# Heads in pairs: scores of the next pair ahead of the transposes of this one, in a two-layer kernel on one core

## What is computed

```python
# layer 0, attention part
xn = rms_norm(x, g_norm) * (1 + scale_b) + shift_b
q, k, v = split(xn @ W_qkv)                  # 512 x 1536
q, k = rms_norm(q, g_q), rms_norm(k, g_k)    # over the 32 values of a head
attn = softmax(q @ k.T * 32 ** -0.5)         # 256 x 256 for each head
o = attn @ v
x1 = o + o @ W_out
# layer 0, feed-forward part, weights from 4-bit codes, scales and a rank-16 term
x2 = relu(x1 @ w_up + b_up) @ w_down + b_down
# layer 1: 256 steps of a Runge-Kutta recurrence with a 512 x 512 coupling,
# x2 as its drive, and a mixture of experts on its states
```

## Time and profile before

| | us |
|---|---|
| median of 3 runs | 2893.96 |
| lowest and highest of them | 2891.05, 2894.92 |
| the profiled execution's own time | 2898.88 |
| its span, from the first to the last instruction | 2897.1 |
| what lies around the span | 1.8 |
| layer 0, to about | 870 |
| layer 1, from there | 2027 |

### The profile page before, as it was taken

One profiled execution on the slowest core, in us unless ns is written; L12 is line 12 of the kernel. 1 busy time (PEld: TensorE's weight loads), 2 busy tenths in 40 slices (PEclk: granted clock), 3 DMA queues, 4 the chain that ended last, 5 costly groups with the idle time before them and its releaser, 6 DMA issues.

```text
span 2897.1 us, 132208 instructions
## 1 busy us (share of the span) xinstructions
PE 2714.9 (94%) x49688; PEld 2397.8 (83%) x49696; DVE 1806.4 (62%) x6366; ACT 1139.6 (39%) x4994; POOL 1364.0 (47%) x3476
## 2 busy tenths in 40 slices
PE   7487988888899999999999999999999999999998
PEld 5265766676687778999999999999999999999987
DVE  4665675565565556666666666666666666666654
ACT  3343345456544333334334333333433433433322
POOL 2422001112116665665666666666666666666600
PEclk8699999999999998999999999999999999999999
DMA  7622344344420003444444444444444444444376
GB/s 218 203 70 70 95 131 144 114 154 159 140 91 3 4 28 98 129 131 131 132 127 135 128 130 129 136 127 127 136 127 129 134 132 128 130 134 130 117 236 201
DMA packets 138459, 363.74 MB, mean 126 GB/s; under 512 B 15968, under 2 KB 25312, under 8 KB 137696
## 3 DMA queue, kind: packets, MB, share of 16 engines
q1 hardware_dynamic: 137568, 357.06, 40.1%
q10 hardware_dynamic: 672, 3.67, 0.3%
HBM read 324.62 MB, written 34.47 MB: 124 GB/s over the span
## 4 chain that ended last, share of the span: by engine, by line
PE 60%; POOL 5%; issue 3%; DVE 2%; DMA 0%; ACT 0%; POOLq 0%; DVEq 0%; SPq 0%
PE pscan L1504 12%; PE pd L1457 12%; PE pg L1409 12%; PE pscan L1500 12%; PE pu L1409 11%; POOL lin L1254 1%; POOL lin L1270 0%; POOL from_q L1266 0%; POOL carry L1299 0%; POOL lin L1264 0%; POOL lin L1276 0%; POOL from_q L1272 0%; POOL from_q L1281 0%; POOL lin L1285 0%; PE prouter L1519 0%
## 5 line engine op out<-in xcount | busy, mean ns | idle before, releaser
L1500 PEld LDWEIGHTS pscan<-th,carry 128*128 128x128 f16 x16384 | 551.1, 96 | 71.7 <-ACT th L1319 50.4
L1500 PE MATMUL pscan<-th,carry 128*128 128x8 f16 x16384 | 560.3, 166 | 19.5 <-ACT th L1319 8.7
L1504 PE MATMUL pscan<-th,carry 128*128 128x16 f16 x16384 | 558.2, 169 | 1.6 <-DVE th L1615 1.1
L1504 PEld LDWEIGHTS pscan<-th,carry 128*128 128x128 f16 x16384 | 482.3, 96 | 2.8 <-DVE th L1615 2.1
L1319 ACT ACTIVATE th<-state 128x32 f16<-128x32 f32 x768 | 175.9, 229 | 688.5 <-DVE state L1632 688.5
L1457 PE MATMUL pd<-hg,wbuf 128*128 128x256 f16 x3168 | 429.3, 274 | 2.6 <-DMA wbuf<-w_split 2.6
L1409 PE MATMUL pg<-qh,wbuf 128*128 128x256 f16 x3168 | 427.3, 274 | 0.0
L1409 PE MATMUL pu<-qh,wbuf 128*128 128x256 f16 x3168 | 423.1, 272 | 0.0
L1632 DVE TENSOR_REDUCE state<-pscan 128x32 f32<-128x96 f32 x768 | 197.7, 257 | 263.2 <-PE pscan L1504 257.4
L1409 PEld LDWEIGHTS pg<-qh,wbuf 128*128 128x128 f16 x3168 | 295.0, 98 | 36.6 <-issue 0.3
L1409 PEld LDWEIGHTS pu<-qh,wbuf 128*128 128x128 f16 x3168 | 292.4, 97 | 31.9
(11 more groups left out here) (273 smaller groups left out, 4774.7 us busy)
## 6 DMA issues: line engine op xcount, KB each, us to landing
wbuf<-w_split SPq DMA_DIRECT2D x264, 512.0 KB, 3.5
wbuf<-w_split SPq DMA_DIRECT2D x264, 384.0 KB, 3.1
parts_mem<-in_w_tiles SPq DMA_DIRECT2D x149, 256.0 KB, 3.2
w_split<-parts_mem SPq DMA_DIRECT2D x99, 256.0 KB, 2.8
late<-in_w_tiles SPq DMA_DIRECT2D x49, 256.0 KB, 3.5
w_split<-spare SPq DMA_DIRECT2D x33, 128.0 KB, 3.1
out<-oo SPq DMA_DIRECT2D x8, 512.0 KB, 3.6
w_qkv<-in_w_qkv ACTq DMA_DIRECT2D x1, 3072.0 KB, 10.0
```

The lines of the kernel that those rows point to most:

```text
L1500: mm(pscan[:, 0, m * B:(m + 1) * B], clo[:, k, m * P:(m + 1) * P], th[:, k, 0, :], start=(m == 0 and k == 0), stop=False, skip_group_check ...
L1504: ins = mm(pscan[:, 0:2, m * B:(m + 1) * B], chi[:, k, m * P:(m + 1) * P], th[:, k], start=False, stop=(k == NC - 1), skip_group_check=True)
```

## The change

The attention stage of layer 0 goes by pairs of heads, p = 0 to 7, in place of groups of four, on PE, ACT and DVE. Each pair uses two of the four banks. PE issues `scores(p + 1)` at the start of pair p, ahead of the transposes of pair p; for it the banks of pair p - 1 must have been copied out. DVE takes the row maxima and ACT the exps of pair p + 1 ahead of the rest of pair p. Each pair has three places for feed-forward parts (`ffn_pair`), one ahead of its first transpose and one behind each.

Beside this ("sister's changes"): `head_norm(c - 1)` is issued between q and k of group c, no longer behind k. The high halves of layer 1's weights (`highs`) of both heads stand behind all relus of the pair; two parts instead of three go to each group of the first stage, the rest to the heads. `hidden_low` of a pair's third place stands behind the next pair's row maxima. The low half of `w_qkv` is made by DVE in one instruction for each of four chunks (`weights_low`) and not by two on POOL; the halves are written in place but for one chunk, for which one DMA is left. The search for the largest entry of `w_qkv` (`widest_qkv`) moves from the start of batch 1 to the end of batch 0. The last half of `second` comes with part 31, and not with part 0 of the next batch. The core of the diff:

```diff
--- before.py
+++ after.py
...
-        high_home = [parts_mem[:, 1536 + 768 * i:1536 + 768 * (i + 1)].bitcast(F16) for i in range(2)]
+        home = parts_mem[:, 3 * N:6 * N]
+        home16 = home.bitcast(F16).rearrange("p (h n) -> p h n", h=2)
+        def split_home(c):
+            return home16 if c == 0 else w16[:, c - 1]
+        def wqkv(k, half, cols):
+            return w16[:, (k + NC - 1) % NC, half, cols]
...
-            return spread((b - 4) * 25, 25, at, 3, PARTS) if b >= 4 else []
+            return spread((b - 4) * 25, 25, at, 2, PARTS) if b >= 4 else []
...
+        ffn_pair = [list(range(5 + 3 * p, 8 + 3 * p)) for p in range(HEADS // 2)]
...
-                    for c in range(NC):
-                        sp.wait_ge(S["w_lo"], c + 1)
-                        sp.dma_start(w16[:, c, 1, :], high_home[c % 2]).then_inc(S["w_back1" if c % 2 else "w_back0"], 16)
+                    sp.wait_ge(S["w_lo"], NC)
+                    sp.dma_start(w_qkv[:, NC - 1, :], home).then_inc(S["w_back"], 16)
...
-                if b == 1:
+                if b == 0:
                     pl.wait_ge(S["w_max"], 1)
                     pl.partition_all_reduce(tops[:, 0:17], tops[:, 0:17], P, bass.bass_isa.ReduceOp.max).then_inc(S["w_all"], 1)
-                    pl.wait_ge(S["w_scale"], 1)
-                    pl.wait_ge(S["p_qk"], SPLIT * NC)
-                    for c in range(NC):
-                        pl.wait_ge(S["w_hi"], c + 1)
-                        pl.tensor_scalar(w_qkv[:, c, :], w_qkv[:, c, :], for_w, None, ALU.mult).then_inc(S["w_scaled"], 1)
-                        pl.wait_ge(S["w_scaled"], c + 1)
-                        pl.tensor_tensor(w16[:, c, 0, :], w_qkv[:, c, :], high_home[c % 2], ALU.subtract).then_inc(S["w_lo"], 1)
...
-                        if c >= 2:
-                            act.wait_ge(S["w_back1" if c % 2 else "w_back0"], 16)
-                        act.activation(high_home[c % 2], w_qkv[:, c, :], ACT.Identity, scale=for_w).then_inc(S["w_hi"], 1)
+                        else:
+                            act.wait_ge(S["w_lo"], c)
+                        act.activation(split_home(c)[:, 1, :], w_qkv[:, c, :], ACT.Identity, scale=for_w).then_inc(S["w_hi"], 1)
                 weights_wide(0)
-                weights_wide(1)
                 def exps(h):
...
-                    highs(NC + h)
...
-                for c in range(NC):
-                    exps(HPC * c)
-                    exps(HPC * c + 1)
-                    if c:
+                exps(0)
+                exps(1)
+                for p in range(HEADS // 2):
+                    c, h = p // 2, 2 * p
+                    if h + 2 < HEADS:
+                        exps(h + 2)
+                        exps(h + 3)
+                    if p % 2 == 0 and c:
                         widened(c - 1)
-                    relus(ffn_quad[c][0:2])
-                    exps(HPC * c + 2)
-                    pieces(HPC * c, 1)
-                    relus(ffn_quad[c][2:3])
-                    exps(HPC * c + 3)
-                    pieces(HPC * c + 1, HPC - 1)
-                    relus(ffn_quad[c][3:])
...
+                        weights_wide(c)
+                    pieces(h, 2)
+                    relus(ffn_pair[p])
+                    highs(NC + h)
+                    highs(NC + h + 1)
...
+                        if c and a == 0:
+                            head_norm(c - 1)
                     ins.then_inc(S["p_qk"], 1)
-                    if c:
-                        head_norm(c - 1)
...
-                def scores(c):
-                    if c == 0:
+                def scores(p):
+                    c = p // 2
+                    if p == 0:
                         pe.wait_ge(S["d_qk"], b * NC + NC)
-                    else:
-                        pe.wait_ge(S["d_pt"], b * HEADS + HPC * c)
+                    if p >= 2:
+                        pe.wait_ge(S["d_pt"], b * HEADS + 2 * p - 2)
                     for qc in range(2):
-                        for j in range(HPC):
-                            r = DH * j
-                            ins = mm(X[j][:, qc * T:(qc + 1) * T], qk[r:r + DH, c, 0, qc * P:(qc + 1) * P], qk[r:r + DH, c, 1, :], start=True, stop=True)
+                        for h in (2 * p, 2 * p + 1):
+                            r = DH * (h % HPC)
+                            ins = mm(X[h % HPC][:, qc * T:(qc + 1) * T], qk[r:r + DH, c, 0, qc * P:(qc + 1) * P], qk[r:r + DH, c, 1, :], start=True, stop=True)
...
-                for c in range(NC):
-                    scores(c)
-                    if c:
+                scores(0)
+                for p in range(HEADS // 2):
+                    c = p // 2
+                    if p + 1 < HEADS // 2:
+                        scores(p + 1)
+                    if p % 2 == 0 and c:
                         weighted(c - 1)
-                    ffn_parts(b, ffn_quad[c][0:2])
-                    for j in range(HPC):
-                        if opening and HPC * c + j + NC < PIECES:
-                            lora(HPC * c + j + NC)
-                        transposed(HPC * c + j)
-                        ffn_parts(b, ffn_quad[c][2 + j:3 + j])
-                        if (c, j) == (1, 1) and more:
-                            norm_sum(b + 1)
+                    places = ffn_pair[p]
+                    ffn_parts(b, places[0:1])
+                    for j in range(2):
+                        h = 2 * p + j
+                        if opening and h + NC < PIECES:
+                            lora(h + NC)
+                        transposed(h)
+                        ffn_parts(b, places[1 + j:2 + j])
+                    if p == 2 and more:
+                        norm_sum(b + 1)
...
+            def weights_low(b, c):
+                if b == SPLIT - 1:
+                    if c == 0:
+                        dve.wait_ge(S["p_qk"], SPLIT * NC)
+                    dve.wait_ge(S["w_hi"], c + 1)
+                    dve.scalar_tensor_tensor(split_home(c)[:, 0, :], w_qkv[:, c, :], for_w, split_home(c)[:, 1, :], ALU.mult, ALU.subtract).then_inc(S["w_lo"], 1)
...
-                if b == SPLIT - 1:
-                    widest_qkv()
...
-                    if h % HPC == 0:
-                        dve.wait_ge(S["p_s"], b * NC + h // HPC + 1)
+                    if h % 2 == 0:
+                        dve.wait_ge(S["p_s"], (b * HEADS + h) // 2 + 1)
...
-                for c in range(NC):
-                    h = HPC * c
-                    row_max(h)
-                    row_max(h + 1)
-                    row_max(h + 2)
-                    if c:
+                row_max(0)
+                row_max(1)
+                for p in range(HEADS // 2):
+                    c, h, places = p // 2, 2 * p, ffn_pair[p]
+                    if h + 2 < HEADS:
+                        row_max(h + 2)
+                        row_max(h + 3)
+                    if p:
+                        lows(b, ffn_pair[p - 1][2:])
+                    if p % 2 == 0 and c:
                         gathered(c - 1)
                     turned(h)
-                    lows(b, ffn_quad[c][0:2])
-                    row_max(h + 3)
+                    lows(b, places[0:1])
+                    if p % 2:
+                        inverse(c)
                     turned(h + 1)
-                    lows(b, ffn_quad[c][2:3])
-                    turned(h + 2)
-                    inverse(c)
-                    turned(h + 3)
-                    lows(b, ffn_quad[c][3:])
-                    if c == 2 and b + 1 < B:
+                    lows(b, places[1:2])
+                    if p % 2:
+                        weights_low(b, c)
+                    if p == 5 and b + 1 < B:
                         normed_input(b + 1)
+                lows(b, ffn_pair[-1][2:])
                 gathered(NC - 1)
+                if b == 0:
+                    widest_qkv()
...
             def lows(b, places):
                 for n, part in ffn_work(b, places):
-                    if part == 0 and n:
-                        second(n - 1, 1)
                     if part < HC and part % 2:
                         hidden_low(n, part // 2)
                     if part == WORK - 4:
                         second(n, 0)
+                    if part == WORK - 1:
+                        second(n, 1)
```

More of the change, by code:

```diff
@@ L169, in layer0 @@
                  "mm_lora scaled stage split d_bounds g_bounds lora_scale lora_high lora_ok "
-                 "w_max w_all w_scale w_hi w_scaled w_lo w_back0 w_back1 "
+                 "w_max w_all w_scale w_hi w_lo w_back "
                  "part_in0 part_in1 part_in2 part_in3 part_out0 part_out1 part_out2 part_hi part_done part_third third_out widest gmax wscale state_in mx par coef setup").split()
@@ L520, in widened @@
                     act.activation(oT[:, c, :], Ob[c % 2][:, T:2 * T], ACT.Copy).then_inc(S["a_wide"], 1)
-                for c in range(NC):
-                    exps(HPC * c)
```

(26 more changed lines are left out.)

4 lines of the change are left out of this document (2 added, 2 removed).

## The result

The changed kernel takes 2977.05 us (median of 4 runs, 2975.89 to 2983.39) where the kernel before took 2894.44 beside it: a ratio of 1.028, 95% interval [1.026, 1.030]. It is slower, as forecast, but by 82.6 us in place of 45.6, and outside the range. The profiled execution has a span of 2976.0 us, 78.9 more than before.

A forecast was written before the change was run, and what follows sets the result against it. The prediction took PE's work and waits (PE busy 94%) as the bound. Its terms summed to +45.6 us on the profiled 2898.9, giving 2944.5; with the median 4.9 below, 2939.6 us (+1.6%), range 2904 to 2960.

The forecast's parts named there:

- scores by pairs: Batches 2 to 7: a pair's scores take as long as four heads', 24 more calls at 1.18 us, +28.3 us.
- first stage, batches 2 to 7: With head_norm between q and k, ACT's square delays the Ln, +0.6 us for each link, +8.4 us in sum.
- waits that go: PE's waits in the attention stages of batches 2 to 7 fall from 46.7 to 20.7 us, -26.0 us.
- the new wait: Batches 4 to 7: scores wait for a copy behind relu, high part and low part, +41.4 us.
- clock: PE's lower clock after waits: about 9 us go, about 11 come, +2 us, bounds 0 to +10.
- w_qkv: Batch 2's 1.46 us wait for the last DMA of these weights goes, -1.5 us.
- batch 1: PE's 8.04 us wait and about 3 us of low clock go, against added scores and waits: net -1 us.
- batch 0: Ring of loads, decoding and splitting gets shorter, -6 us, bounds -15 to +3.
- The rival of cheap scores: A pair's scores cost 0.54 us, all else unchanged: 2911 us, chance 0.12.
- no new chain: The 41.4 us of waits don't come, as relus are done before PE needs the copy: 2898 us, chance 0.06.
- faster: Hand-overs between engines set the pace, not PE's work; dearer scores lie in kept waits: 2869 us, chance 0.08.
- Longer stalls: Each relu-to-copy chain takes 1 us more and is followed by low clock: 2961 us, chance 0.12.

The follow-up runs named there:

- The two cuts of the chain: Two runs of the changed kernel: low parts issued behind both copies, 2936.12 us; high parts issued ahead of the relus, 2953.78 us.
- with groups of four: Changed kernel with PE, ACT and DVE back to the attention loops of the kernel before, all else kept: 2896.81 us, ratio 0.9997.
- cured pairs: Changed kernel with low parts behind both copies, and Ln and Exp ahead of the next square: 2898.67 us, ratio 0.9999.
- the two edits that were worth 26 us together: Kernel before with only head_norm's matmul between q and k, and Ln and Exp ahead of the next square: 2870.79 us, ratio 0.9915.

## Why the prediction was right or wrong

The forecast's terms against the two traces, by stages (us):

| term | forecast | measured |
| --- | --- | --- |
| scores by pairs | +28.3 | +19 without the 0.10 of going over to them: a pair 1.06; the first two pairs of a batch run side by side, 1.10; 6 x (1.10 + 6 x 1.06 - 4 x 1.08) |
| first stage, batches 2 to 7 | +8.4 | +4.2: head_norm +9.6, one high part less -5.4 |
| waits that go | -26.0 | -11.0: of 36.1 us ahead of the attention stage's instructions 25.1 stay |
| the new wait | +41.4 | +41.3 |
| clock | +2 | +22: the 71.6 of six attention stages less the rows above that lie in them (19 - 11.0 + 41.3) |
| w_qkv | -1.5 | -1.6 |
| batch 1 | -1 | +8.3: first stage +0.6, attention 56.68 to 64.37 |
| batch 0 | -6 | -3.7: loads -1.3, attention 82.06 to 77.26, `w_out` at a lower clock +2.3 |
| sum | +45.6 | +79 |

**The new wait** was right in mechanism, place and size. At the pairs that the forecast names it measured 7.5, 9.3, 10.2 and 9.7 us in batches 4 to 7 (forecast 8.2, 10.1, 11.1, 12.0), and 4.7 more at pairs that it doesn't name. The two cuts of the chain show its cause.

**Clock** is the term that failed, and the largest error: it was put at +2 us, with 10 as its upper bound, and is +22. I had priced the low clock at 11 us behind the new waits and set 9 against it for the waits that go. The 22 is what is left over in the table, and the granted clocks bear it out: the traces' records of it hold two levels only, 1.00 and 0.50, so a stage at a mean clock of c spends 2 x (1 - c) of its time at 0.50, which makes some 22 us of the six attention stages before and some 71 in the changed kernel. Half of the 49 more is some 25 us, less what of it is waiting. PE's busy time says the same, 41.6 us more, of which 19 are scores. Some 2 us of the 22 can be the 0.10 of the 18 more times that PE goes over to scores. The prediction's 2.4 GHz is the higher level as the trace of before shows it, 2.4 columns a ns: 24 products of 512 columns take 5.18 us (351.52 to 356.70) and 48 of 256 take 5.24 (356.70 to 361.94), 256 columns more are 0.107 us, and the granted clock is 1.00 in both. Its 1.2 GHz is half of that, for a granted clock of 0.50: 12 matmuls of 256 columns take 2.54 us at it (742.00 to 744.54 in the changed kernel), 1.2 columns a ns, and 1.31 at 1.00 (766.48 to 767.79).

Neither half of the forecast held. The new waits cost about twice my 11: each of the four that were filled gave back 2.8 us on average, some three quarters of its own length. And the 9 us weren't given back. In the kernel before, the clock fell to 0.50 once in each of the six attention stages, half of these behind waits that I took out (2.20 in batch 2, 2.41 in batch 3, 3.17 in batch 4). The waits stayed or others came (3.28 in batch 2, 4.04 in batch 4), and it fell as before. Behind the first transposes, a wait that I had expected to shrink, it is now 0.50 in five batches, where it was in two. Short waits cost nothing of this kind in these traces: the eight of 0.5 to 1.7 us ahead of scores in batches 4 to 7 are each followed by scores of 1.13, at full clock.

**Waits that go** is the second. The first transposes still wait 15.8 us for the exps, where I had 9.1. Two things were wrong there. PE is at them 2.6 us after the first scores and not 3.5, since the first two pairs' scores run side by side: what the scores saved, these waits took back in part. And in batch 5 the maxima start 3.7 us after the first scores (614.36), behind two `hidden_low` and two low parts, where they started 4.3 after before: the low part less freed 0.7 us of DVE and not 1.6. Waits for `hidden_low` in batches 2 and 3 (3.3 us at the longest), for copies there (3.8 in all) and ahead of `weighted` stayed too.

**Batch 1** is the third. The wait of 8.04 went as forecast, but the row maxima behind it were not free of DVE's other work (a low half of 1.81 us, then `normed_input`), and other waits came: with groups of four the stage gained 2.7 us, not 11. What the pairs cost in it, 10.3 us (54.03 to 64.37), the forecast had nearly right with some 10: scores, and waits of 2.44, 1.89, 2.25 and 4.18 for exps and copies. It was the gain that was a quarter of its forecast.

**Scores** were read rightly from the one row: the chain of a quarter holds for one head, two and four (1.06, 1.06 and 1.10 us). Of that time four passes of 256 columns explain some 0.86 by an estimate from the 0.216 us of a float32 instruction of `w_out` (18 in 3.88 us, 347.64 to 351.52 before, granted clock 1.00); what takes the other 0.2, the prediction's ramp, no run shows. I had not seen that the first two pairs of a batch follow one another in different quarters and so cost one call. The rival of cheap scores is out. That each change of tiling waits for the last matmul's tail, as the prediction sets beside its sum, was not shown: a part ahead of scores takes 1.40 us in the changed kernel (768.23 to 769.63), ahead of a transpose 1.31 (766.48 to 767.79), the same 0.10 as before, and the 5.3 us more didn't come.

**The first stage** was right for head_norm (9.6 for the links), and high since one high part less saves 5.4 us and not 2.4. **The other rivals**: no new chain and faster have fallen by the timeline. Longer stalls (2961) was nearest, but half by luck: the stalls were not longer (41.3 us for 41.4), the low clock behind them was, and of that it had only 8 us.

Not settled in full: why cured pairs stay 39 us behind groups of four. Of the 37.7 us in the attention stages of batches 2 to 7 the scores explain 19 and waits 3. The granted clocks are 0.92 to 0.97 against 0.97 to 1.00, which by the same working is some 35 us more at 0.50 and up to 17 of loss, enough for the rest. But no run tried that by itself, and why the clock falls more often with pairs, at waits of nearly the same sum (43.7 and 40.8 us), is open.

## What to carry to other kernels

Price a wait of PE with what it does to the clock: take from the trace the time of the same instructions behind a short and a long wait, and put that difference behind each long wait that an edit brings or takes. Before an instruction that another engine needs at once, look at what stands ahead of it in its own queue: one low part between two copies tied the scores to a relu, and one square ahead of a Ln held a link back by 1.9 us. An edit that moves an instruction on one engine should be costed with the order of the queue that it feeds, since the two edits that were worth 26 us together were worth nothing or less alone.

## What the runs showed of the hardware

That work of no use can make a kernel faster: 106 matmuls put into four waits of 3.2 to 4.3 us took 8.5 us off by the medians (11 by the ratios), since the instructions behind ran at a granted clock of 1.00 and not 0.50. That waits of 2.8 to 2.9 us, ahead of the first transposes, were each followed by a granted clock of 0.50 in five batches of five. And that in these row-tiled products the time is that of the fullest quarter: 4, 8 and 16 instructions of 256 columns took 1.06, 1.06 and 1.10 us. The fastest version found, groups of four with the matmul of squares between q and k and the Ln ahead of the next square, takes 2859.36 us, 0.9875 of the kernel before.
